# Counting the selection flag of a top-k threshold as a product of two columns, in a fused LayerNorm and sparse feed-forward kernel

## The reference, cut to what matters

```
x = layernorm(x + x @ (W + delta_W).T)                 # 4096 tokens of 512
z = x @ ternary(W_syn).T + b_syn                       # 4096 x 2048
k = 204                                                # 2048 * (1 - 0.9)
thresh = top_k(z, k)[:, -1:]                           # the 204th largest of each row
hidden = where(z >= thresh, relu(z), 0)
out = hidden @ ternary(W_out).T + b_out
y = layernorm(layernorm(x + out) * gamma + beta + x)   # both with eps 1e-5
```

## Time and profile before

| | us |
|---|---|
| median of 3 runs (lowest, highest) | 650.38 (649.47, 650.42) |
| profiled execution, whole time | 649.1 |
| profiled execution, span of the trace | 647.2 |
| PE busy | 586.9 (91%) |
| DVE busy | 551.2 (85%) |
| ACT busy | 550.5 (85%) |
| POOL busy | 374.6 (58%) |

### The profile page before, as it was taken

One profiled execution on the slowest core, in us unless ns is written; L12 is line 12 of the kernel. 1 busy time (PEld: TensorE's weight loads), 2 busy tenths in 40 slices (PEclk: granted clock), 3 DMA queues, 4 the chain that ended last, 5 costly groups with the idle time before them and its releaser, 6 DMA issues. The chain is left out here.

```text
span 647.2 us, 8553 instructions
## 1 busy us (share of the span) xinstructions
PE 586.9 (91%) x2482; PEld 266.0 (41%) x2482; DVE 551.2 (85%) x655; ACT 550.5 (85%) x723; POOL 374.6 (58%) x712
## 2 busy tenths in 40 slices
PE   8798769899999999999999999999999999886553
PEld 7443324344444444444444444444444444332211
DVE  5786988989999999899889999999999999998751
ACT  1888558998999999999999999999999999988631
POOL 1126385667666666666666666666666666666631
PEclk9999789999999999999999999999999999999787
DMA  8971234545555453556564545445354554453350
GB/s 338 325 230 50 49 82 82 114 98 115 98 102 115 86 112 82 114 92 131 98 131 97 118 95 126 102 84 112 81 109 89 99 98 99 97 83 81 81 99 32
DMA packets 184514, 71.64 MB, mean 111 GB/s; under 512 B 168080, under 2 KB 176272, under 8 KB 183824
## 3 DMA queue, kind: packets, MB, share of 16 engines
q1 hardware_dynamic: 184464, 71.07, 50.0%
HBM read 20.72 MB, written 8.39 MB: 45 GB/s over the span
## 5 line engine op out<-in xcount | busy, mean ns | idle before, releaser
L530 ACT ACTIVATE junk<-z_sb,t_col 128x2048 f16<-128x2048 f32 x128 | 254.9, 1992 | 9.0 <-POOL t_col L427 8.0
L942 PE MATMUL z_ps<-t_syn,xhT 128*128 128x512 f16 x1024 | 231.0, 379 | 2.7 <-DVE t_syn L650 2.7
L942 PEld LDWEIGHTS z_ps<-t_syn,xhT 128*128 128x128 f16 x1024 | 99.9, 98 | 134.2 <-issue 18.1
L954 PE MATMUL o_ps<-t_out,hT 128*128 128x512 f16 x512 | 122.3, 394 | 23.6 <-DMA hT<-hh 18.7
L408 POOL TENSOR_SCALAR tmp<-signs,dev 128x1 f32<-128x1 f32 x64 | 48.5, 758 | 149.8 <-ACT junk L530 149.8
L925 PE MATMUL u_ps<-weff,xT_sb 128*128 128x512 f32 x256 | 117.3, 601 | 2.4 <-ACT x1s L549 2.4
L960 PE MATMUL o_ps<-t_out,hT 128*128 128x512 f16 x512 | 117.5, 383 | 0.0
L820 DVE SCALAR_TENSOR_TENSOR z_sb<-z_sb,thr 128x2048 f32<-128x2048 f32 x32 | 75.3, 2352 | 28.2 <-DVE flag L799 26.7
L566 ACT ACTIVATE hh<-z_sb,sc 128x2048 f16<-128x2048 f32 x32 | 64.1, 2002 | 33.9 <-DVE z_sb L820 33.9
L954 PEld LDWEIGHTS o_ps<-t_out,hT 128*128 128x128 f16 x512 | 51.3, 101 | 90.1 <-DMA hT<-hh 20.7
L786 DVE SCALAR_TENSOR_TENSOR z_sb<-z_ps,sc,bias_z 128x1024 f32<-128x1024 f32 x64 | 81.9, 1279 | 4.4 <-PE z_ps L942 4.4
(11 more groups left out here) (118 smaller groups left out, 585.2 us busy)
## 6 DMA issues: line engine op xcount, KB each, us to landing
xT_sb<-in_xT SPq DMA_DIRECT2D x16, 512.0 KB, 4.8
out_y<-y_sb SPq DMA_DIRECT2D x32, 256.0 KB, 2.8
z_sb<-in_w_synT SPq DMA_DIRECT2D x4, 1024.0 KB, 12.4
hh<-in_w_outT SPq DMA_DIRECT2D x2, 1024.0 KB, 10.0
z_sb<-in_w_outT SPq DMA_DIRECT2D x2, 1024.0 KB, 10.7
weff<-in_wT SPq DMA_DIRECT2D x2, 512.0 KB, 4.8
w_sb<-in_dwT SPq DMA_DIRECT2D x2, 512.0 KB, 5.7
bias_z<-in_b_syn SPq DMA_DIRECT2D x1, 1024.0 KB, 5.7
```

The lines of the kernel that those rows point to most:

```text
L530: a_.activation(junk[:, n % 2, :], z_sb[:, t % ZS, :], ACT.Sign, bias=at, scale=-1.0, accum_out=signs[:, j, r:r + 1]).then_inc(counted, 1)
L942: last = mm(z_ps[:, c, b * BANK:(b + 1) * BANK], xhT[:, j, h * KD + k, :], t_syn[:, k, n0:n0 + BANK], start=k == 0 and h == 0, stop=k == K ...
L954: mm(o_ps[t % OS][:, :], hT[:, j, 0, c, :], t_out[:, c, :], start=c == 0, stop=False)
```

## The change

`ok` goes. In its place VectorE makes a column `under` (largest of `m8` less than the trial) in a new step `guard`, directly behind `top8`. The count of good rows, formerly ones times `ok`, becomes the matmul of `hit` (stationary) with `under` (moving), whose sum over the 128 partitions is the same number. TensorE waits for both columns. The two semaphores `guarded` and `hit_made` replace `selected`; `thr_made` now counts only the thresholds, and the two places on ScalarE and GpSimd that waited for `selected` of the tile two before wait for `thr_made` of it.

```diff
-                    wait(pool, selected, t - 1)
+                    wait(pool, thr_made, t - 1)
...
-                        wait(act, selected, t - 1)
+                        wait(act, thr_made, t - 1)
...
+            def guard(t):
+
+                j = t % 2
+                dve.wait_ge(max8_done, t + 1)
+                v.tensor_scalar(less[:, j:j + 1], m8[:, j, 0:1], t_col[:, j, ROUNDS - 1:ROUNDS], None, ALU.is_lt, ALU.add,
+                                accum_out=under[:, j:j + 1]).then_inc(guarded, 1)
+
             def select(t):
 
                 j = t % 2
                 said = signs[:, j, ROUNDS - 1:ROUNDS]
-                dve.wait_ge(max8_done, t + 1)
-                dve.wait_ge(counted, count_no(t, 4))
+                dve.wait_ge(counted, count_no(t, ROUNDS - 1))
                 v.tensor_scalar(pick[:, j, :], place[:, :], said, None, ALU.is_equal, ALU.add,
-                                accum_out=hit[:, j:j + 1]).then_inc(thr_made, 1)
-                dve.wait_ge(thr_made, 2 * t + 1)
-                v.scalar_tensor_tensor(ok[:, j:j + 1], m8[:, j, 0:1], t_col[:, j, ROUNDS - 1:ROUNDS], hit[:, j:j + 1],
-                                       ALU.is_lt, ALU.mult).then_inc(selected, 1)
+                                accum_out=hit[:, j:j + 1]).then_inc(hit_made, 1)
+                dve.wait_ge(guarded, t + 1)
+                dve.wait_ge(hit_made, t + 1)
                 v.scalar_tensor_tensor(pick[:, j, :], place[:, :], said, m8[:, j, :],
                                        ALU.is_equal, ALU.mult, accum_out=thr[:, j:j + 1]).then_inc(thr_made, 1)
...
             def hidden(t):
-                dve.wait_ge(thr_made, 2 * t + 2)
+                dve.wait_ge(thr_made, t + 1)
...
                     below(f)
                     top8(f)
+                    guard(f)
...
             def flags(t):
 
-                pe.wait_ge(selected, t + 1)
+                pe.wait_ge(guarded, t + 1)
+                pe.wait_ge(hit_made, t + 1)
                 wait(pe, flag_read, t)
                 if t >= OS:
                     pe.wait_ge(z_evac, 2 * upto(t + 1))
-                mm(flag_at(t), ones[:, 0:1], ok[:, t % 2:t % 2 + 1], start=True, stop=True).then_inc(flag_ready, 1)
+                mm(flag_at(t), hit[:, t % 2:t % 2 + 1], under[:, t % 2:t % 2 + 1], start=True, stop=True).then_inc(flag_ready, 1)
```

More of the change, by code:

```diff
@@ L126, in postln_kernel @@
         hit = sb("hit", [P, 2])
-        ok = sb("ok", [P, 2])
+        under = sb("under", [P, 2])
+        less = sb("less", [P, 2])
         flag = sb("flag", [1, 1], I32)
@@ L202, in postln_kernel @@
         thr_made = sem("thr_made")
-        selected = sem("selected")
+        guarded = sem("guarded")
+        hit_made = sem("hit_made")
         flag_ready = sem("flag_ready")
@@ L874, in _ @@
             top8(0)
+            guard(0)
             out_weights(1)
```

## The result

The change makes the kernel slower. The median is 651.98 us (651.28 to 652.30 in 11 runs) against 650.38 for before (647.76 to 650.89 in 11 runs beside it), a ratio of 1.0033 with an interval of 1.0021 to 1.0045. The forecast was 648.5 us, so the direction is wrong, and 651.98 lies above the range's upper end of 651.4. The profiled execution took 651.93 us. Its span is 650.14 us, against 647.17 before: 3.0 us more.

The account below looks back on a forecast made before the run. PE was taken to bound the steady stretch; its end moves by -0.76 - 1.48 = -2.2 us, with the drain about 2.5, of which 1.9 arrives: 648.5 us on the median of 650.38, range 646.8 to 651.4.

Parts of the forecast that it names:

- What bounds the kernel, and the 0.2 us of slack: From about 140 to 559 us PE sets the pace at 17.47 us a stage; DVE has 0.2 us of slack.
- the second rival: DVE cycle becomes the bound as guard pushes `lo_x` back; about 650.4 us at +0.25, 653 at +0.35; chance 0.17.
- DVE, guard: Guard directly behind MAX8 moves `lo_x` and the end of the GpSimd sum L382 by 0.25 us each.
- DVE, select: Threshold step ends with the GpSimd sum; `centre` comes 0.11 us later per stage, bounds -0.14 and +0.25.
- Does DVE keep up?: DVE cycle becomes 17.38 us, under 17.47; 1.3 us behind, DVE gains 0.09 a stage, level after some 15 stages.
- PE, flags: Flags matmul keeps its shape; the extra semaphore wait costs 0, bounds 0 to 1.2 us over 24 stages.
- PE, release in the ramp, and the clock: At tile 3's flag PE starts 0.76 us earlier; idle 1.9 us keeps the clock at 2.4 GHz, saving 1.48 us.
- The drain: Last four stages: one +0.11 us, three together -0.3; last tile's mm3 starts about 2.5 us earlier, 1.9 us arriving.
- The first and the third rival: First: clock falls all the same, 649.6 us, chance 0.28; third: half-rate stretch takes the gain back, 650.4 us, chance 0.10.

Follow-up runs that it names:

- code moved: The changed kernel with 80 more DVE instructions that never run inside tile 3's slow search, so later instructions lie elsewhere; measured 651.81 us, ratio 1.0042.

## Why the prediction was wrong

*What bounds the kernel, and the 0.2 us of slack.* Right (the first window has DVE at 14.86, 2.6 us of air and not 1 to 2). The point from which the second rival decides was put at +0.20 us on DVE, and the measured addition was +0.29.

*DVE, guard.* `lo_x` +0.26, predicted +0.25; the sum's end +0.27, predicted +0.25. Right, and L382 did not go first in any stage of after.

*DVE, select.* +0.14 up to `centre`, predicted +0.11, bounds -0.14 and +0.25. `centre` starts 0.05 us before the sum's end, where before it started 0.08 behind it, as the missing step should make it. Three hundredths short, inside its bounds.

*Does DVE keep up?* This is the step that failed. It took the cycle for 17.27 + 0.11 = 17.38, and 17.56 was measured: of the 0.18 missing, 0.13 are the register load, 0.03 `centre` and 0.02 the rest. It left all that lies behind `centre` at its length in before. That included the stretch from the reading of the flag to `hidden`, 0.86 us, which was taken for a constant. It held a register load whose length depends on how far behind the transpose of `xh` it starts. Guard moved `lo_x`, and so the transpose, 0.26 us later, but the reading of the flag of an unheld DVE only by 0.14, from 7.29 to 7.43 us after the mask. The distance fell from 2.13 to 2.00 us, and the load grew by 0.13. `lo_x` releases a DMA, and nothing in the working asked what that DMA would run beside once it came later. Tile 0 of before, with 1.50 us in the place of 0.86 and no releaser, was the row that should have raised the question, though part of its length has another cause. The kernel with the transpose behind the flag is the counter-test: with a short load the cycle is 17.41, under PE's 17.47, and the 23 stages cost nothing.

*PE, flags.* Predicted 0, bounds 0 to 1.2 us. Right: in the kernels where PE sets the pace the stage is 17.47, with both waits and two fresh operands. In after the gap ahead of the flag is PE waiting for `hit`.

*PE, release in the ramp, and the clock.* Tile 3 of after, and the window behind it, against the earlier trace rows:

```profile
126.24 0.19 PE L979 MATMUL z_ps<-under,hit 128*1 128x1 f32 x2 [2.02 <-DVE less L770]
126.36 3.63 PE L969 MATMUL o_ps<-t_out,hT 128*128 128x512 f16 x16
```

```profile
126.20:129.80 3.60, 3.56 (x18) 1.70 (x19) 2.58 (x5) 3.53 (x4) 1.30 (x2) 1.00 0.39 73
```

The row names `less`, but that had been made 0.85 us before; it was `hit`, whose reading of the accumulator ended at 126.13. PE starts 0.24 us earlier, not 0.76. The cycles of tiles 0, 1 and 2 grew by 0.19, 0.06 and 0.10 us and delayed the mask of tile 3 by 0.35, where 0.1 was booked; tile 2 was left out of that sum, and its growth is that of its register load (0.401 against 0.303). 0.24 more came from the setup. The idle stretch is 2.02 us, close to the 1.9 forecast, and the group takes 3.63: the fall is gone, and its 1.48 us with it, as forecast for this execution. As far as the runs show that was luck: in two other kernels with about the same idle stretch the clock fell (last section). And it was worth nothing. PE's lead is of use only where PE sets the pace, and from tile 3 on DVE does.

*The drain.* Tiles 29 to 31 have `centre` 0.12 to 0.13 us earlier each (6.39, 6.39 and 6.24 us after the mask), together 0.37 where 0.42 was forecast. Tile 28 cost 0.66, where 0.11 was forecast: 0.28 for its longer cycle, and a late start of 0.38. Tile 31 starts 0.32 late. From `hidden` of tile 31 to the end 0.58 us came back, with a mean granted clock of 0.78 against 0.74 in before.

*The second rival* is what happened, though with a mechanism only half its own. Its arithmetic holds up: +0.29 instead of +0.25 gives (17.56 - 17.47) x 23 = 2.1 us, less the 0.8 of the ramp which did not come either. It had a chance of 0.17, too little: the room under PE's pace was 17.47 - 17.38 = 0.09 us (the margin of 0.17 us that it names is the room before L382 would go first), in a sum in which one stretch of 0.86 us had not been taken apart. The first and the third rival did not decide: in this trace the clock stayed up behind the flag of tile 3, and the loss arose in the steady stretch, not at the end.

*Late starts.* In no row of before, and not foreseeable from it: 1.4 us of the 3.0 up to tile 28, and 0.32 in tile 31. They are in the code of the kernels with guard behind `lo_x` as well (tiles 19, 22, 25, 28 and 31 again). There PE's pace covers the first three: DVE loses 0.38 in tile 19, PE's flags stay 17.47 apart.

## To carry to other kernels

When an engine has a tenth or two of slack, take apart every stretch of its cycle that the views call idle, register loads and branches among them, before adding to it. Put a short added step where the engine would otherwise wait for another (here behind `lo_x`, beside the GpSimd sum: 0.26% faster than before instead of 0.33% slower), not ahead of the instruction that releases a GpSimd turn and a DMA. And an earlier start on the bounding engine is worth only what the next engine can follow.

## What the runs showed of the hardware

**A register load is delayed by a DMA transpose.** DVE's load of one word from on-chip memory took 0.30 to 0.32 us where no transpose had been issued in the 2.1 us ahead of it, 0.42 to 0.46 us when it began 2.0 us after the issue of the transpose of `xh`, and 0.77 to 0.90 us when it began 1.2 to 1.3 us after (0.74 once). In tile 1, where it began 0.5 to 0.8 us after the issue, it took 0.31 to 0.32: it was over at 1.11 us, before the first packet at 1.17. Moving the transpose behind the load brought it back to 0.30 to 0.32 in every tile but tile 0, which kept 0.55, in both kernels where that was done. The length does not follow the packets beside the load (0.305 us at 288 GB/s, 0.425 at 2 GB/s), so the means are open. The Trainium skill says that a DMA never contends with a compute engine ("SBUF — State Buffer", Who interferes with whom). For the compute instructions the traces agree: `centre` takes 0.75 us beside the transpose and away from it. For the load that the engine's sequencer makes they do not.

**`hidden` can start 0.30 to 0.38 us late behind a branch**, mostly in every third tile over some stretch, and the tiles change when code that never runs is added. Without the guard it was tiles 2, 5, 8 and so on to 26; with the guard added to before 7, 10, 21 and 24; in before, none. A packet of instructions begins 0.6 to 2.8 us behind each late branch.

**The clock's fall is not decided by the idle time alone.** Behind the flag of tile 3 it fell to 1.2 GHz after idle stretches of 2.75 us (before), 1.92 (transpose behind the flag), 2.07 (no guard) and 3.40 (before with guard); it stayed at 2.4 GHz after 2.02 (after), 2.00 (code moved), and 1.79, 1.81 and 1.80 (the three with guard behind `lo_x`). All five that stayed up have the two-column flag, but so has one that fell; what else differs was not tried. So what the prediction expected, no fall after some 1.9 us, came true in after for reasons that stay open.
